# Four edge layers of a graph network: run sums kept as blocks of first runs, written by GpSimd

## The chip, the cores and the metric

One core of a Trainium2 chip runs the whole program in one launch. The metric is the device time of one execution in microseconds (us). Smaller is better.

## The reference, cut to what matters

The network works on 50000 nodes with 256 values each and on 25000 edges (`src`, `dst`), sorted by `dst`. Four sub-networks follow each other, each with a residual and a layer norm: a hypergraph network, two graph-attention layers with four heads, a graph convolution with batch norm, and two more attention layers. An edge layer takes the row of every edge's source, weighs it and sums over all edges with the same target:

```python
alpha = ex / denom[dst]
msg = h[src] * alpha[:, :, None]
out = jax.ops.segment_sum(msg, dst, num_segments=n)
```

Edges with one target lie side by side. Such a stretch is called a run here, and its sum a run sum.

## The kernel before, in words

The edges lie on 128 partitions (`P`), 196 in a row on each (`C`), cut into 25 batches (`NBAT`) of 8 columns (`BC`). The last batch has 4. Five layers have edges: l1, l2 (attention, in the class `Nodes` the kinds `l1a` and `l1b`), l3 (convolution, `gcn`), l5 and l6 (attention, `l3a` and `l3b`). A batch norm stands between l3 and l5.

The class `Edges` does the edges of a layer. GpSimd (POOL) gathers the source rows of a batch, one indirect DMA for each column into one of three buffers `eg` (L1804). VectorE (DVE) weighs them (L2008, in l3 L1995) and adds them up along the partition into one of three buffers `erun` (L2024): element k of a partition is the sum of its run up to k. At the batch's end DVE raises `s_run`. In the attention layers ScalarE (ACT) then copies the running maxima beside the sums (L1876) and raises `s_mc`. SyncE (SP) waits for that and stores the whole batch, 128 partitions by 8 columns, in a DRAM table (L1828): `GSUMS` in l1, l2, l5, `SUMS` in l3, and `GSUMS1` in l6. The buffer is free for a new batch when `s_sv` tells that the store has landed.

A run that goes on from one partition to the next has to be joined. After the last batch, POOL waits for all stores and gathers one row for each partition, the sum of its first run, by the index `repair32` (L1812, tile `hp`). PE multiplies it by a matrix that carries it to the partition before (l3: L1842), and DVE adds it to the last run there (`join`). Nothing else reads the stored sums. A partition whose first run doesn't continue one of the partition before has the index 60000, which is out of bounds, and such rows are left out of a gather or scatter. In the data of the reference 41 of the 128 partitions start inside a run; in 40 of them that run ends within the first 8 columns, in one within the second 8.

The class `Nodes` does the tiles of 512 nodes beside it: 49 that own the targets (region 0) and 49 others (region 1). All engines follow one list of ticks. In a tick POOL first issues what `Edges.gpsimd` gives it, then what `Nodes.gpsimd` gives it, and waits in that order. In l2 and l5 that is a reciprocal square root for two tiles (L2340, tile `rs`). In l5, POOL also has the square roots of the region-1 tiles that are finished in the same layer (L2348, tile `vrs`), which DVE waits for in `moved_shifts` (L2733), and the scatter of their rows to the output (L2356, four for a tile), which wait for ACT to normalize them (`l_v`).

Every layer, and the setup ahead of the first, is a block: no engine starts the next one before all are done. In the setup SP issues loads, the first 40 pieces that clear the table `NS0` (L191), and three stores of zeros (L326, L327), and then waits until these have landed.

```python
for b in range(NBAT):
    if tick == (self.copy_at(b) + 1 if self.heads else self.at(b) + 2):
        if self.heads:
            sp.wait_ge(self.s_mc, b + 1)
        else:
            sp.wait_ge(self.s_run, b + 1)
        sp.dma_start(self.accv[:, b * BC:b * BC + WIDTH[b], :], self.run[b % self.nrun][:, 0:WIDTH[b], :]).then_inc(self.s_sv[b % self.nrun], 16)
```

Of the kernel before, what the change touches and what calls it, by code (L numbers as in the profile page):

```python
# [225 lines left out]
def setup_phase(nc, S, V, A, T, early):  # L226
    with Scope(nc, "su") as s:
# [64 lines left out]
        s_pad = s.sem("pad_rows_ready")  # L292
        s_ps = s.sem("pad_rows_stored")
        with s.block() as block:

            @block.sync
            def _(sp):
# [33 lines left out]
            @block.gpsimd
            def _(pool):
# [56 lines left out]
            def _(dve):  # L389
# [27 lines left out]
                dve.tensor_copy(small[:, 2:3], hpos[:])  # L417
                dve.memset(S["same"][:, 0:1], 0.0)
# [122 lines left out]
                dve.sem_inc(s_cw, 1)  # L541
                dve.memset(S["row_a"][:], 0.0)
# [1160 lines left out]
class Edges:  # L1703


    def __init__(self, nc, S, s, table, tw, index, acc, heads, first, slots, load=None, bias=None):
# [5 lines left out]
        self.aw, self.sumw = acc.shape[1], D + H  # L1712
        self.accv = acc.rearrange("(p c) w -> p c w", c=C)
# [5 lines left out]
        self.s_sv = s.sems("runs_stored", self.nrun)  # L1719
# [1272 lines left out]
```

## Time and profile before

| | |
|---|---|
| median of 3 runs | 6476.59 us (6467.43 to 6479.67) |
| the profiled execution, span from first to last instruction | 6468.6 us |
| PE, DVE, ACT, POOL busy | 4325.2, 4671.1, 3126.0, 3855.5 us |
| l1, batches | 2703 to 3119 us |
| l2, batches | 3266 to 3847 us |
| l3, batches | 3960 to 4325 us |
| l5, batches | 5063 to 5703 us |
| moved by DMA | 1558.35 MB |

The page gives no other time of the profiled execution than its span. The stages run one after another and have different limits, so an engine's share of the whole span tells little. Each stage has to be read by itself: which engine has no idle time there, and what the others wait for.

### The profile page before, as it was taken

How to read it: one execution, taken by the hardware profiler on the slowest of the kernel's cores; microseconds unless marked ns; L12 is line 12 of the kernel's file. 1: busy time of each engine (PE TensorE's matmuls, PEld its weight loads, DVE VectorE, ACT ScalarE, POOL GpSimd, SP SyncE). 2: the span in 40 equal slices, each digit the busy share in tenths (PEclk: the TensorE clock that was granted, in tenths of full speed). 3: DMA queues.
4: the chain of work that ended last, by engine and by line, in shares of the span. 5: the costliest groups of instructions: out<-in, count | busy, mean ns of one | idle time of the engine just before them, and what ended most of it. 6: DMA issues, size and time to landing. Idle time of an engine off the chain costs nothing. (4 is left out here: it accounts for less than half of the span.)

```text
span 6468.6 us, 75458 instructions
## 1 busy us (share of the span) xinstructions
PE 4325.2 (67%) x19189; PEld 3131.7 (48%) x19189; DVE 4671.1 (72%) x15403; ACT 3126.0 (48%) x6788; POOL 3855.5 (60%) x3139
## 2 busy tenths in 40 slices
PE   2668884038886899588876667997898477790000
PEld 1257773037775677477622223555777355560000
DVE  6645454745554877599599986977888899957776
ACT  0023331013332566488655556765776377782333
POOL 4767775767886577666155524741111688747776
PEclk9689997569998899799977778998999788895555
DMA  8845545974443898799688878998998687756665
GB/s 301 311 125 78 79 75 101 388 230 77 79 78 52 288 312 302 243 326 319 222 292 295 304 264 307 399 338 300 342 347 302 213 287 275 276 213 224 236 237 199
DMA packets 616396, 1558.35 MB, mean 241 GB/s; under 512 B 126988, under 2 KB 283090, under 8 KB 599038
## 3 DMA queue, kind: packets, MB, share of 16 engines
q1 hardware_dynamic: 430270, 1159.75, 51.2%
q0 software_dynamic: 185696, 393.77, 22.6%
q8 instruction: 158, 2.59, 0.2%
q14 instruction: 272, 2.23, 0.1%
HBM read 794.19 MB, written 811.66 MB: 248 GB/s over the span
## 5 line engine op out<-in xcount | busy, mean ns | idle before, releaser
L859 POOL DMA_INDIRECT NS<-e_tot,e_idx x392 | 658.9, 1681 | 232.7 <-ACT e_tot L1122 91.6
L1804 POOL DMA_INDIRECT l_eg<-HBT,k_nsrc x392 | 484.4, 1236 | 352.3 <-POOLq L160 120.6
L993 DVE TENSOR_SCALAR e_eq<-e_pk,z_skey 128x128 f32<-128x128 f32 x588 | 203.6, 347 | 621.0 <-DMA NS<-e_tot,e_idx 590.4
L2410 PE MATMUL l_pm<-k_w_L3b,l_zt 128*128 128x258 f32 x1568 | 412.4, 423 | 124.3 <-ACT l_o L2469 123.8
L1257 POOL DMA_INDIRECT XH<-n_o,z_home x392 | 384.3, 980 | 165.0 <-issue 113.1
L2384 PE MATMUL l_ps<-l_a,k_ident 128*128 128x512 f32 x392 | 308.4, 879 | 227.1 <-DVE l_a L2662 215.9
L2548 ACT ACTIVATE l_a<-l_a,l_eshare 128x64 f32<-128x64 f32 (+1 forms) x980 | 280.5, 372 | 311.6 <-DVE l_eshare L2066 311.6
L2024 DVE SCALAR_TENSOR_TENSOR l_erun<-l_erun,k_same,l_eg 128x260 f32<-128x260 f32 (+2 forms) x880 | 415.4, 472 | 3.0
L2410 PEld LDWEIGHTS l_pm<-k_w_L3b,l_zt 128*128 128x128 f32 x1568 | 327.0, 214 | 186.2 <-issue 133.0
L2410 PE MATMUL l_pm<-k_w_L1b,l_zt 128*128 128x264 f32 x1568 | 380.9, 398 | 54.1 <-ACT l_o L2469 53.8
L2739 DVE BATCH_NORM_STATS2 l_bs<-l_a 128x6 f32<-128x256 f32 x1016 | 402.3, 413 | 1.3
L1511 POOL TENSOR_TENSOR n_rs<-n_ve,k_minus_half 128x8 f32<-128x8 f32 x49 | 80.2, 1636 | 520.9 <-DVE n_ve L1669 520.9
L1847 PE MATMUL l_pb<-l_jx,k_ones 128*128 128x128 f32 x26 | 5.2, 351 | 560.7 <-DVE l_jx L2084 560.7
L1068 PE MATMUL e_po<-z_w_e2n,e_hid 128*128 128x256 f32 x1584 | 375.9, 380 | 2.8 <-DVEq L956 2.8
L1077 PE MATMUL e_pr<-e_zt,z_w_n2e 128*128 128x256 f32 x1584 | 377.2, 381 | 0.7 <-ACT e_hid L1142 0.7
L1281 PE MATMUL n_pm<-z_w_L1a,n_zt 128*128 128x264 f32 x1568 | 370.5, 390 | 0.0
L1548 PE MATMUL n_pm<-k_w_L3a,n_zt 128*128 128x264 f32 x1568 | 367.7, 388 | 0.1
L1804 POOL DMA_INDIRECT l_eg<-XH,k_psrc x196 | 255.4, 1303 | 177.9 <-DVEq L2029 119.0
L2497 ACT ACTIVATE l_z<-l_a,l_nb,l_rs 128x256 f32<-128x256 f32 x624 | 321.9, 588 | 78.2 <-DVE l_nb L2803 69.6
L2401 PE MATMUL l_pm<-l_zt,k_w_L 128*128 128x512 f32 x784 | 354.2, 595 | 0.0
L2410 PEld LDWEIGHTS l_pm<-k_w_L1b,l_zt 128*128 128x128 f32 x1568 | 298.3, 195 | 113.2 <-issue 64.6
L1068 PEld LDWEIGHTS e_po<-z_w_e2n,e_hid 128*128 128x128 f32 x1584 | 301.6, 191 | 45.2 <-issue 3.5
(443 smaller groups left out, 13326.7 us busy)
## 6 DMA issues: line engine op xcount, KB each, us to landing
HBT<-l_o SPq DMA_DIRECT2D x196, 528.0 KB, 4.3
l_a<-HBT SPq DMA_DIRECT2D x156, 528.0 KB, 6.2
GSUMS<-l_erun SPq DMA_DIRECT2D x72, 1056.0 KB, 6.0
NS<-z_zero SPq DMA_DIRECT2D x100, 520.0 KB, 5.9
l_a<-XH SPq DMA_DIRECT2D x98, 528.0 KB, 6.1
HA<-n_o SPq DMA_DIRECT2D x98, 528.0 KB, 4.5
l_a<-HA SPq DMA_DIRECT2D x98, 528.0 KB, 6.3
X<-l_z SPq DMA_DIRECT2D x98, 520.0 KB, 7.7
```

The lines of the kernel that those rows point to most:

```text
L859: pool.indirect_dma_start(out=nodes, out_offset=bass.IndirectOffsetOnAxis(ap=idx[q % DEEP][:, k:k + 1], axis=0), in_=tot[q % 2][:, k, :], ...
L1068: mm = pe.matmul(po[:, k, :], hid[q % 2][:, i, k * P:(k + 1) * P], w2[:, i, 0:D], start=i == 0, stop=i == KC - 1)
L1077: mm = pe.matmul(pr[:, n, :], w1[:, i, n * P:(n + 1) * P], zt[q % 2][:, i].rearrange("p j n -> p (j n)"), start=i == 0, stop=i == KC - 1)
L1257: pool.indirect_dma_start(out=T["XH"], out_offset=bass.IndirectOffsetOnAxis(ap=S["home32"][:, col:col + 1], axis=0), in_=o[t % RO][:, j, : ...
L1281: last = pe.matmul(pm[h][:, i, 0:RW], zt[t % 2][:, k, h * (J // 2) + i, :], weight[:, k, :], start=k == 0, stop=k == KC - 1)
L1548: last = pe.matmul(pm[h][:, i, 0:RW], zt[t % 2][:, k, h * (J // 2) + i, :], weight[:, k, :], start=k == 0, stop=k == KC - 1)
L1804: pool.indirect_dma_start(out=self.g[b % self.ng][:, k, :], out_offset=None, in_=self.table, in_offset=bass.IndirectOffsetOnAxis(ap=self.i ...
L2024: lk.link(dve.scalar_tensor_tensor(rt[:, k, 0:n], before, S["same"][:, b * BC + k:b * BC + k + 1], g[:, k, 0:n], ALU.mult, ALU.add))
L2401: last = pe.matmul(self.pm[u % 2][:, m, :], self.weight[:, k, m * P:(m + 1) * P], zt[:, k].rearrange("p j n -> p (j n)"), start=k == 0, st ...
L2410: last = pe.matmul(self.pm[h][:, i, 0:self.wc], zt[:, k, h * (J // 2) + i, :], self.weight[:, k, 0:self.wc], start=k == 0, stop=k == KC - 1)
L2497: last = act.activation(z[:, j, 0:D], a[:, j, 0:D], ACT.Identity, bias=self.nb[b][:, col:col + 1], scale=self.rs[b][:, col:col + 1])
L2739: self.stat_lk.link(dve.bn_stats(bs[:, u % 2 * J + j, :], a[:, j, 0:D]))
```

## The change

In l1, l2, l3 and l5 (`kept=True`) SP no longer stores the batches. For each batch POOL issues one indirect DMA in its place. It writes the 8 columns of a partition, one piece of 8448 bytes (8192 in l3), to row p of a small table (`HEADRUNS`, `HEADSUMS`), for those partitions alone whose first run continues one from the partition before and ends in this batch (`headblock32`). All other indices are out of bounds. The write waits for `s_mc` (in l3 `s_run`), as the store did, and stands in POOL's order ahead of the gathers of its tick. The gather for the join reads the row in that block (`headrow32`). The setup works out the two indices on DVE, and SP clears the two tables at the end of its list, with five more DMAs that the setup waits for. l6 stays as it was.

```diff
@@ setup, SP
                 sp.dma_start(T["SUMS"][PC:PC + 1, :], pad[0:1, 0:D]).then_inc(s_ps, 16)
+                zero = S["zero"][:].rearrange("p r c -> p (r c)")
+                for table in (T["HEADRUNS"], T["HEADSUMS"]):
+                    for c in range(0, table.shape[1], CLEAR * SW):
+                        w = min(CLEAR * SW, table.shape[1] - c)
+                        sp.dma_start(table[:, c:c + w], zero[:, 0:w]).then_inc(s_hz, 16)
                 sp.wait_ge(s_pre, 16)
                 sp.wait_ge(s_ps, 16 * 3)
+                sp.wait_ge(s_hz, 16 * 5)
@@ setup, POOL
+                pool.iota(block32[:], [[BC, NBAT]], base=0, channel_multiplier=0).then_inc(s_iota, 1)
+                pool.iota(part32x[:], [[1, 1]], base=0, channel_multiplier=BC).then_inc(s_iota, 1)
@@ setup, DVE
+                dve.tensor_copy(colblock[:], block32[:])
+                dve.tensor_copy(part8[:, 0:1], part32x[:])
...
+                dve.tensor_scalar(part8[:, 1:2], small[:, 0:1], -1.0, None, ALU.add)
+                dve.tensor_scalar(part8[:, 2:3], small[:, 0:1], float(-BC), None, ALU.add)
+                dve.drain()
...
+                dve.tensor_copy(S["headblock32"][:], colblock[:])
...
+                dve.tensor_scalar(S["headrow32"][:], part8[:, 3:4], float(NONE), None, ALU.add)
@@ class Edges
-        self.aw, self.sumw = acc.shape[1], D + H
-        self.accv = acc.rearrange("(p c) w -> p c w", c=C)
+        self.aw, self.sumw = acc.shape[1] // BC if kept else acc.shape[1], D + H
+        self.kept = kept
+        self.accv = None if kept else acc.rearrange("(p c) w -> p c w", c=C)
...
-        self.s_sv = s.sems("runs_stored", self.nrun)
+        self.s_sv = [s.pool_sem(S, f"head_runs_kept{b}") for b in range(self.nrun)] if kept else s.sems("runs_stored", self.nrun)
...
+    def kept_at(self, b):
+        return self.copy_at(b) + 1 if self.heads else self.at(b) + 2
@@ Edges.gpsimd, in the loop over the batches, behind the gathers of a batch
+            if self.kept and tick == self.kept_at(b):
+                if self.heads:
+                    pool.wait_ge(self.s_mc, b + 1)
+                else:
+                    pool.wait_ge(self.s_run, b + 1)
+                pool.indirect_dma_start(out=self.acc, out_offset=bass.IndirectOffsetOnAxis(ap=self.S["headblock32"][:, b:b + 1], axis=0),
+                                        in_=self.run[b % self.nrun][:].rearrange("p k w -> p (k w)"), in_offset=None,
+                                        bounds_check=P - 1, oob_is_err=False).then_inc(self.s_sv[b % self.nrun], 16)
@@ Edges.gpsimd, the join
-            pool.indirect_dma_start(out=self.hp[:, :], out_offset=None, in_=self.acc,
-                                    in_offset=bass.IndirectOffsetOnAxis(ap=self.S["repair32"][:], axis=0),
-                                    bounds_check=PC - 1, oob_is_err=False).then_inc(self.s_hp, 16)
+            if self.kept:
+                pool.indirect_dma_start(out=self.hp[:, :], out_offset=None, in_=self.acc.rearrange("p (k w) -> (p k) w", k=BC),
+                                        in_offset=bass.IndirectOffsetOnAxis(ap=self.S["headrow32"][:], axis=0),
+                                        bounds_check=P * BC - 1, oob_is_err=False).then_inc(self.s_hp, 16)
...
@@ Edges.sync
-            if tick == (self.copy_at(b) + 1 if self.heads else self.at(b) + 2):
+            if not self.kept and tick == self.kept_at(b):
@@ gnn_kernel
-        "GSUMS": nc.dram_tensor("GSUMS", (PC, RW), F32).ap(),
+        "HEADRUNS": nc.dram_tensor("HEADRUNS", (P, BC * RW), F32).ap(),
+        "HEADSUMS": nc.dram_tensor("HEADSUMS", (P, BC * D), F32).ap(),
```

Line numbers of the changed kernel are larger by some 40 to 52: the gather L1804 is L1843 there, the new write L1852, the gather for the join L1860, and L2340, L2348, L2356 are L2392, L2400, L2408.

POOL in the middle of l5, before (`l_eg` the gathers of edge rows, `l_rs` and `l_vrs` the square roots, `out_dram<-l_v` the scatter to the output):

```order
L2340 TENSOR_TENSOR l_rs<-l_ve,k_minus_half 128x8
L2356 DMA out_dram<-l_v,k_ids 50000x256 x4
L1804 DMA l_eg<-HA,k_nsrc 128x264 x2
L2348 TENSOR_TENSOR l_vrs<-l_vve,k_minus_half 128x8
L2356 DMA out_dram<-l_v,k_ids 50000x256 x4
L1804 DMA l_eg<-HA,k_nsrc 128x264 x2
L2340 TENSOR_TENSOR l_rs<-l_ve,k_minus_half 128x8
L1804 DMA l_eg<-HA,k_nsrc 128x264 x6
L2340 TENSOR_TENSOR l_rs<-l_ve,k_minus_half 128x8
```

The same place in the changed kernel:

```order
L2392 TENSOR_TENSOR l_rs<-l_ve,k_minus_half 128x8
L2408 DMA out_dram<-l_v,k_ids 50000x256 x4
L1852 DMA HEADRUNS<-l_erun,k_headblock 128x2112
L1843 DMA l_eg<-HA,k_nsrc 128x264 x2
L2400 TENSOR_TENSOR l_vrs<-l_vve,k_minus_half 128x8
L2408 DMA out_dram<-l_v,k_ids 50000x256 x4
L1843 DMA l_eg<-HA,k_nsrc 128x264 x2
L2392 TENSOR_TENSOR l_rs<-l_ve,k_minus_half 128x8
L1843 DMA l_eg<-HA,k_nsrc 128x264 x4
L1852 DMA HEADRUNS<-l_erun,k_headblock 128x2112
L1843 DMA l_eg<-HA,k_nsrc 128x264 x2
L2392 TENSOR_TENSOR l_rs<-l_ve,k_minus_half 128x8
```

Two writes have come in, each behind the first two gathers of a batch and ahead of the others. All that follows on POOL stands behind them, the square root `l_vrs` among it.

POOL at the end of l3, before:

```order
L1804 DMA l_eg<-X,k_nsrc 128x260 x196
L1812 DMA l_hp<-SUMS,k_repair 128x256
L2842 UNCONDITIONAL_BRANCH
L1496 UNCONDITIONAL_BRANCH
L1499 TENSOR_TENSOR n_bt<-n_bmv,k_minus_half 128x2
```

And in the changed kernel:

```order
L1843 DMA l_eg<-X,k_nsrc 128x260 x6
L1852 DMA HEADSUMS<-l_erun,k_headblock 128x2048
L1843 DMA l_eg<-X,k_nsrc 128x260 x6
L1852 DMA HEADSUMS<-l_erun,k_headblock 128x2048 x3
L1860 DMA l_hp<-HEADSUMS,k_headrow 128x256
```

The last three writes of the layer stand on POOL right ahead of the gather for the join, where POOL before had nothing but the wait for SP's stores.

## Rows read from the trace of the kernel before

**Rows 1.** Windows by stage (l1, l2, l3, l5): length, busy (instructions), clock, DMA share, GB/s.

```profile
2703.00:3119.00 416.00, 363.49 (x1852) 306.14 (x1851) 408.37 (x850) 346.68 (x944) 226.55 (x169) 0.98 0.94 321
3266.00:3847.00 581.00, 396.13 (x644) 119.16 (x645) 564.74 (x1540) 347.17 (x940) 287.37 (x209) 0.75 0.87 297
3960.00:4325.00 365.00, 365.00 (x1358) 198.94 (x1358) 316.48 (x606) 265.82 (x531) 233.90 (x187) 1.00 1.01 386
5063.00:5703.00 640.00, 478.38 (x2051) 348.41 (x2052) 597.03 (x1864) 439.68 (x949) 497.39 (x365) 0.84 0.78 274
```

**Rows 2.** DMA issues: the run stores that go (count, KB each, us to landing).

```profile
GSUMS<-l_erun SPq DMA_DIRECT2D x72, 1056.0 KB, 6.0
SUMS<-l_erun SPq DMA_DIRECT2D x24, 1024.0 KB, 6.8
...
GSUMS<-l_erun SPq DMA_DIRECT2D x3, 528.0 KB, 4.1
```

**Rows 3.** Groups of POOL's DMAs in l1, l2, l3, l5: busy, mean ns | idle, releasers.

```profile
L1804 POOL DMA_INDIRECT l_eg<-XH,k_psrc x169 | 226.6, 1341 | 146.0 <-DVEq L2029 100.9 <-issue 45.1
L1804 POOL DMA_INDIRECT l_eg<-HBT,k_nsrc x171 | 225.1, 1316 | 152.7 <-DVEq L2029 103.2 <-issue 42.2 <-ACT l_z L2497 7.3
L1804 POOL DMA_INDIRECT l_eg<-X,k_nsrc x172 | 218.1, 1268 | 92.3 <-issue 46.3 <-DVEq L2029 46.0
L1804 POOL DMA_INDIRECT l_eg<-HA,k_nsrc x178 | 224.6, 1262 | 73.0 <-issue 48.6 <-DVEq L2029 23.5 <-ACT l_a L2497 0.9
L2356 POOL DMA_INDIRECT out_dram<-l_v,k_ids x128 | 163.2, 1275 | 47.8 <-issue 34.6 <-ACT l_v L2533 12.9 <-ACT l_a L2497 0.3
```

**Rows 4.** Waits of DVE in l5's batches: us in total, times, longest.

```profile
DVE l_vnb L2733 <- POOL l_vrs L2348: 38.2, 11, 5.7
```

**Rows 5.** Timeline of l5, POOL and DVE: start, duration, [idle before <- releaser].

```profile
5173.09 1.02 POOL L1804 DMA_INDIRECT l_eg<-HA,k_nsrc  x1 [8.59 <-DVEq L2029]
...
5222.02 0.17 DVE L2733 SCALAR_TENSOR_TENSOR l_vnb<-l_vmv,l_vrs 128x8 f32<-128x8 f32 x1 [3.67 <-POOL l_vrs L2348]
...
5392.55 0.17 DVE L2733 SCALAR_TENSOR_TENSOR l_vnb<-l_vmv,l_vrs 128x8 f32<-128x8 f32 x1 [3.66 <-POOL l_vrs L2348]
...
5447.09 1.02 POOL L2356 DMA_INDIRECT out_dram<-l_v,k_ids  x1 [2.69 <-ACT l_v L2533]
...
5513.66 1.02 POOL L1804 DMA_INDIRECT l_eg<-HA,k_nsrc  x1 [2.26 <-DVEq L2029]
...
5631.19 0.17 DVE L2733 SCALAR_TENSOR_TENSOR l_vnb<-l_vmv,l_vrs 128x8 f32<-128x8 f32 x1 [1.36 <-POOL l_vrs L2348]
```

**Rows 6.** The two scatters by `repair32` (L841), 41 of 128 rows: issue to landing.

```profile
DMA to landing us min/median/max: 2.3/3.6/4.8
```

**Rows 7.** The scatter that adds in DRAM, from the page's groups: busy, mean ns.

```profile
L859 POOL DMA_INDIRECT NS<-e_tot,e_idx x392 | 658.9, 1681 | 232.7 <-ACT e_tot L1122 91.6
```

**Rows 8.** Timeline of l3's join on SP, POOL and PE.

```profile
4317.67 0.66 SPq L1828 DMA_DIRECT2D SUMS<-l_erun  x1
...
4325.61 1.00 POOL L1812 DMA_INDIRECT l_hp<-SUMS,k_repair  x1 [35.11 <-DMA SUMS<-l_erun]
...
4323.93 1.04 PE L2440 MATMUL l_pt<-k_ident,l_a 128*128 128x128 f32 x8
...
4328.24 1.04 PE L2440 MATMUL l_pt<-k_ident,l_a 128*128 128x128 f32 x8
4331.95 0.70 PE L1842 MATMUL l_pc<-l_hp,k_joinT 128*128 128x256 f32 x2 [2.67 <-DMA l_hp<-SUMS,k_repair]
...
4337.61 1.04 PE L2440 MATMUL l_pt<-k_ident,l_a 128*128 128x128 f32 x8
```

**Rows 9.** The setup's end: a window by its DMA, SP's last store, DVE's next instruction.

```profile
80.00:94.00 14.00, 0.00 (x0) 0.00 (x0) 4.11 (x13) 0.00 (x0) 0.00 (x0) 1.00 1.03 410
...
96.63 0.21 SPq L327 DMA_DIRECT2D SUMS<-su_pad  x1
...
106.27 0.91 DVE L877 MEMSET e_run<- 128x1024 f32 x1 [21.62 <-PEq L160]
```

More of the change, by code:

```diff
@@ L541, in _ @@
                 dve.sem_inc(s_cw, 1)
+                dve.tensor_scalar(part8[:, 1:2], small[:, 0:1], -1.0, None, ALU.add)
+                dve.tensor_scalar(part8[:, 2:3], small[:, 0:1], float(-BC), None, ALU.add)
+                dve.drain()
+                dve.tensor_scalar(inblock[:], colblock[:], part8[:, 1:2], None, ALU.is_le)
+                dve.tensor_scalar(colblock[:], colblock[:], part8[:, 2:3], small[:, 3:4], ALU.is_ge, ALU.mult)
+                dve.tensor_scalar(part8[:, 4:5], part8[:, 0:1], 1.0 / BC, float(-NONE), ALU.mult, ALU.add)
+                dve.drain()
+                dve.tensor_tensor(inblock[:], inblock[:], colblock[:], ALU.mult)
+                dve.drain()
+                dve.tensor_scalar(colblock[:], inblock[:], part8[:, 4:5], float(NONE), ALU.mult, ALU.add)
+                dve.drain()
+                dve.tensor_copy(S["headblock32"][:], colblock[:])
+                dve.tensor_tensor(inblock[:], inblock[:], V["iota"][:, 0:NBAT], ALU.mult)
+                dve.drain()
+                dve.tensor_reduce(part8[:, 3:4], inblock[:], AX_X, ALU.add)
+                dve.tensor_tensor(part8[:, 1:2], part8[:, 1:2], part8[:, 0:1], ALU.add)
+                dve.drain()
+                dve.scalar_tensor_tensor(part8[:, 3:4], part8[:, 3:4], float(-BC), part8[:, 1:2], ALU.mult, ALU.add)
+                dve.drain()
+                dve.tensor_scalar(part8[:, 3:4], part8[:, 3:4], float(-NONE), small[:, 3:4], ALU.add, ALU.mult)
+                dve.drain()
+                dve.tensor_scalar(S["headrow32"][:], part8[:, 3:4], float(NONE), None, ALU.add)
                 dve.memset(S["row_a"][:], 0.0)
@@ L1703, with __init__ @@
 class Edges:
-    def __init__(self, nc, S, s, table, tw, index, acc, heads, first, slots, load=None, bias=None):
+    def __init__(self, nc, S, s, table, tw, index, acc, heads, first, slots, load=None, bias=None, kept=False):
         self.bias, self.s_ad = bias, s.sem("target_logits_biased")
@@ L1811, in gpsimd @@
                 pool.wait_ge(self.s_sv[b], 16 * len(range(b, NBAT, self.nrun)))
-            pool.indirect_dma_start(out=self.hp[:, :], out_offset=None, in_=self.acc,
-                                    in_offset=bass.IndirectOffsetOnAxis(ap=self.S["repair32"][:], axis=0),
-                                    bounds_check=PC - 1, oob_is_err=False).then_inc(self.s_hp, 16)
+            if self.kept:
+                pool.indirect_dma_start(out=self.hp[:, :], out_offset=None, in_=self.acc.rearrange("p (k w) -> (p k) w", k=BC),
+                                        in_offset=bass.IndirectOffsetOnAxis(ap=self.S["headrow32"][:], axis=0),
+                                        bounds_check=P * BC - 1, oob_is_err=False).then_inc(self.s_hp, 16)
+            else:
+                pool.indirect_dma_start(out=self.hp[:, :], out_offset=None, in_=self.acc,
+                                        in_offset=bass.IndirectOffsetOnAxis(ap=self.S["repair32"][:], axis=0),
+                                        bounds_check=PC - 1, oob_is_err=False).then_inc(self.s_hp, 16)
     def landed(self, b):
@@ L2951, in gnn_kernel @@
         layer_phase(nc, S, "l1", dict(kind="l1a", rows=h1, rw=RW, weight=S["w_L1b"], out=T["HBT"], self_act=2, slots=FIRST),
-                    dict(table=pairs, tw=RW, index=S["psrc32"], acc=T["GSUMS"], load=asd), first=12)
+                    dict(table=pairs, tw=RW, index=S["psrc32"], acc=T["HEADRUNS"], kept=True, load=asd), first=12)
         layer_phase(nc, S, "l2", dict(kind="l1b", rows=T["HBT"], rw=RW, resid=x1, out=T["X2"], self_act=2, slots=FIRST),
-                    dict(table=T["HBT"], tw=RW, index=S["nsrc32"], acc=T["GSUMS"], bias=S["logit_b"]), first=12)
+                    dict(table=T["HBT"], tw=RW, index=S["nsrc32"], acc=T["HEADRUNS"], kept=True, bias=S["logit_b"]), first=12)
         with Scope(nc, "y") as y:
```

11 lines of the change are left out of this document (7 added, 4 removed).

## The prediction, on record before the run

> **What bounds the kernel now.** I read the windows by stage first, since the change touches four stages with different limits. In l1 VectorE (DVE) works 408.37 of 416 us and in l2 564.74 of 581; in l3 the matmul engine (PE) works 365 of 365 [rows 1]. These three have an owner that hardly ever rests. In l3 the beat shows it: from one tile's transposes to the next, 4323.93 to 4328.24, are 4.31 us [rows 8].
>
> l5 is different. DVE has 597.03 us of work in 640, and GpSimd (POOL) 497.39 [rows 1]; but POOL also spends 48.6 and 34.6 us on issuing between its DMAs [rows 3], so it is taken for 580.6 of 640 us. The waits say who waits for whom: DVE stood 38.2 us, 11 times, for a square root on POOL [rows 4]. The timeline shows the loop. POOL gets its last long rest at 5173.09 (8.59 us); from then on DVE waits for it again and again, first at 5222.02, last at 5631.19. The same wait, 3.67 and 3.66 us long, comes back after 5392.55 - 5222.02 = 170.5 us, which is six batches. In such a period POOL itself rests only twice, 2.69 us for ScalarE (ACT) and 2.26 us for the end of a batch on DVE, and both are echoes of its own lateness [rows 5]. So from 5173 to 5631 the chain that sets the pace runs mostly through POOL's list.
>
> DMA is the third view. The stores that go are 72 x 1056 KB and 24 x 1024 KB [rows 2], some 103 MB of the 1558 MB moved. The DMA share is 0.94 in l1 and 1.01 in l3 [rows 1], yet DVE in l1 and PE in l3 don't stop for DMA within the batches. Only at the end of l3 does PE wait for one [rows 8].
>
> **The change, part by part.** What it removes: 25 stores in each of four layers. None of them is waited for before the join, so in the batches they are worth 0. The bound below is the 7.6 us of l1 in which DVE is idle and the 16.3 us of l2, if all of it were made by crowded loads; I take 0, since an owner that is busy 97% and more leaves its rests to other causes too.
>
> What it adds in l1, l2 and l3: one indirect DMA on POOL per batch, with the gathers of the next batch behind it. A scatter costs 1275 ns in l5 plus 34.6/128 = 0.27 us of issuing [rows 3], so 1.55 us. POOL's rests for the end of a batch are 100.9, 103.2 and 46.0 us over some 21 batches [rows 3], that is 4.8, 4.9 and 2.2 us per batch. Each is larger than 1.55, so the write fits in: 0. If the cover failed it would fail first in l3, by at most 25 x 0.5 = 12 us if the price were 2.7. In l1 and l2 the write also waits for ACT's copy of the maxima, and POOL's gathers behind it; this eats rest of the same kind.
>
> l5: here the writes come on top of a full list. By the order rows each stands behind the first two gathers of a batch, and twice between one `l_vrs` and the next. From 5173 to 5631 are 458 us, or 458/170.5 x 6 = 16 batches, so 16 writes. One of six, the one just ahead of the 2.69 us rest, is swallowed by it; that happens three times. The other 13 push `l_vrs`, DVE behind it and the next batch behind DVE: 13 x 1.55 = **+20.1 us**. From below: a price of 1.02 + 0.27 = 1.29 us (the short scatter at 5447.09 [rows 5]), 16.8 us for 13, and if the rests of 2.69 (three) and 2.26 (two) could all be filled, 12.6 less, 4.2. From above: all 16 at the price of the scatter that adds, 1681 ns [rows 7], plus 0.27: 31.2. I take 20.1, by the rows of the same stage.
>
> A scatter's length is not its own. In l5 its mean is 1275 ns, a quarter above the 1.02 us of a short one [rows 3, 5]; what lengthens the others is left open here, and the mean carries it into the sum. The Trainium skill (SBUF — State Buffer, Who interferes with whom) says that a DMA issued from SP is free of DVE, while GpSimd, which writes descriptors itself, is kept out by some DVE instructions. By its figure for a blocked one, about 3.1 us, 13 writes would cost an estimated 13 x 3.4 = 44 us. The rows of l5 don't show such a mean, so the sum stays with them.
>
> The join of l3: the last store is issued at 4317.67, and POOL's gather starts at 4325.61 [rows 8], 7.9 us later. The write would be issued at about the same moment, since both wait for the same semaphore, and land 3.6 us later (2.3 to 4.8) [rows 6]. The gather then comes some 4 us earlier, more than the 2.67 us that PE waits for it. The tile in which PE waits takes 4337.61 - 4328.24 = 9.37 us in place of 4.31, and PE has no slack to make it up: **-5.1 us**, 0 at the least. In the joins of l1, l2 and l5 the half batch's store lands in 4.1 us [rows 2] against 3.6 [rows 6]: 0, from -2 to +1 together.
>
> The setup: DVE is done long before its end and rests 21.62 us up to 106.27 [rows 9], so its extra arithmetic is hidden, and ends later only if it took longer than that. What DVE waits for is SP's list of clears. SP's last store stands at 96.63; the DMA engines move 410 GB/s ahead of it, which is all they reach in this program's stages. The five new clears are 128 x (2112 + 2048) x 4 = 2.13 MB behind that: 2.13/410 = **+5.2 us**, with nothing beside it. At l1's 321 GB/s it would be 6.6; if the last transfers' tail hid part, 3.
>
> **The sum**: +20.1 - 5.1 + 5.2 = +20.2 us on the profiled span of 6468.6, so 6488.8. The median of the runs shown, 6476.59, lies 8 us above that span; with the same difference the forecast is **6497 us**.
>
> **The rivals.**
>
> *POOL's rests take the writes.* If the 2.69 and 2.26 us are room and no echo, l5 costs 4 to 10 us and the time is 6476.6 + 5.2 + 7 - 5.1 = 6484: no change that can be told. For it: DVE itself is idle for 43 us in l5, so neither engine is full. Against it: DVE's wait and POOL's rest follow each other in the same period, as links of one chain. It decides when l5 grows by less than 13.
>
> *Traffic is what paces the stages* (this one ends faster). If loads and gathers arrive late because 1 MB stores crowd them, l3 would shorten by its stores' 25 MB at 386 GB/s, 65 us, or by any part of it; with a tenth of that and 10 us from l1 and l2 the sum is 6476.6 + 20.2 - 6.5 - 10 = 6480, and from a quarter of l3's on with l1's and l2's idle time the kernel is faster: 6476.6 + 20.2 - 16 - 24 = 6457. The Trainium skill (SBUF — State Buffer, A bandwidth-pool intuition that's wrong) holds that HBM is almost always the bottleneck from end to end. The shares of 0.94 and 1.01 speak for it. Against it stand the owners' full windows and the beat of 4.31 us.
>
> *The list of POOL gets longer than planned.* At 1681 ns for each write and with l3's POOL falling behind, 6476.6 + 5.2 + 31 + 5 = 6518. The price of a scatter whose rows are nearly all out of bounds is not in the trace by itself.
>
> *The writes do next to nothing.* Should an indirect DMA without a valid row be skipped in well under 1 us, l5 costs under 8 us: 6482.
>
> **How the numbers follow.** A measurement of this kernel can tell about 0.2% (13 us) from no change. The forecast gets 0.50 (6489 to 6509), the longer list 0.14, both slower. POOL's rests 0.22 and the cheap write 0.04: same. The traffic 0.10: faster. That is slower 0.64, same 0.26, faster 0.10. The range of 6470 to 6518 leaves out most of the faster case and the far end of the longer list.
>
> **What would show it.** In the changed profile: SP's run stores gone and some 100 MB less moved; POOL's new group of 25 for each layer, at 1.0 to 1.6 us; in l5 DVE's wait for `l_vrs` well above 38.2 us and the six-batch period near 178 us in place of 170.5; in l3 PE's beat unbroken at the join; the first DVE instruction of the next block near 111.5. The prediction is wrong if l5's period stays at 170 us, if the writes take under 0.7 us or over 2, or if l1 or l2 change by more than 5 us.

## The result, and the profile after

The changed kernel takes 6487.07 us (median of 15 runs, 6474.70 to 6489.53). The kernel before, beside it and with 15 runs too, takes 6467.43 us. The ratio is 1.0027 (95% interval 1.0020 to 1.0034), so the change costs 19.6 us by the medians and 13 to 22 us by the interval. Forecast were 6497 us and +20.2 us: slower, as expected, and by the expected amount. The 10 us between 6497 and 6487 are nearly all the starting point: the three runs known then had a median of 6476.59, fifteen have 6467.43. But the right sum hides a wrong term and one that was not seen, and these are what this part is about.

The profiled execution has a span of 6483.0 us against 6468.6. It splits by the first VectorE (DVE) instruction of each block. (A second profile of the kernel before stands in the table, to show how far two profiles of one kernel differ. The columns are us, the differences are taken before rounding, and the forecast is by stage.)

| stage | before | before, again | after | after - before | forecast |
|---|---|---|---|---|---|
| setup | 106.3 | 106.7 | 111.3 | +5.0 | +5.2 |
| hypergraph layers, first nodes | 2541.5 | 2549.6 | 2543.7 | +2.3 | 0 |
| l1 | 565.4 | 563.4 | 569.9 | +4.6 | 0 |
| l2, to l3's first tile | 746.0 | 746.0 | 744.6 | -1.5 | 0 |
| l3 | 428.0 | 429.2 | 422.8 | -5.2 | -5.1 |
| batch norm | 647.0 | 647.2 | 646.6 | -0.4 | 0 |
| l5 | 793.4 | 790.3 | 801.6 | +8.1 | +20.1 |
| l6 | 641.0 | 641.8 | 642.6 | +1.5 | 0 |

The unchanged second stage took between 2529 and 2551 us in the twelve profiles of this case, so a few us there say nothing. l3 with the write in it and the batch norm repeat to 1 us, l2 to some 6 (744.1 to 750.2). l1 falls into two groups: 563.4 to 566.1 us in the four profiles in which it stores, 569.7 to 570.1 in the eight in which it writes.

The windows by stage, as in [rows 1] (length, then busy time of PE, PEld, DVE, ACT, POOL, clock, DMA share, GB/s):

```profile
2711.00:3127.00 416.00, 365.86 (x1856) 308.49 (x1856) 408.78 (x850) 346.83 (x940) 269.98 (x195) 0.97 0.83 260
3279.00:3860.00 581.00, 395.57 (x643) 118.90 (x643) 563.46 (x1538) 345.97 (x937) 310.45 (x233) 0.75 0.79 252
3970.00:4335.00 365.00, 365.00 (x1357) 198.98 (x1356) 318.20 (x607) 264.97 (x530) 252.65 (x213) 1.00 0.96 316
5064.00:5717.00 653.00, 475.89 (x2059) 347.65 (x2060) 599.32 (x1874) 441.56 (x952) 519.88 (x392) 0.84 0.67 223
```

The stores are gone: in l1 the DMA rate falls from 321 to 260 GB/s, in l3 from 386 to 316. The owners of l1 to l3 do the same work in the same length. PE is busy 365 of 365 us in l3 with or without 25 MB of stores, so the traffic did not pace that stage. Only l5's stretch is longer, 653 us for the 640 of before, with DVE's work unchanged.

The groups of POOL's DMAs, as in [rows 3] (busy, mean ns | idle before them, what ended it), of l1, l2, l3 and, from the fourth row on, l5:

```profile
L1852 POOL DMA_INDIRECT HEADRUNS<-l_erun,k_headblock x25 | 35.8, 1431 | 46.1 <-ACT l_erun L1928 40.0 <-issue 6.1
...
L1852 POOL DMA_INDIRECT HEADRUNS<-l_erun,k_headblock x25 | 37.0, 1481 | 55.9 <-ACT l_erun L1928 53.3 <-issue 2.6
...
L1852 POOL DMA_INDIRECT HEADSUMS<-l_erun,k_headblock x25 | 30.9, 1238 | 50.5 <-DVEq L2081 47.2 <-issue 3.4
...
L1843 POOL DMA_INDIRECT l_eg<-HA,k_nsrc x180 | 217.9, 1210 | 65.1 <-issue 48.5 <-DVEq L2081 14.2 <-ACT l_erun L1928 1.5
L1852 POOL DMA_INDIRECT HEADRUNS<-l_erun,k_headblock x25 | 33.6, 1343 | 7.3 <-issue 7.0 <-ACT l_a L2549 0.3
```

In l1 to l3 the writes took over the rest that the gathers had: POOL now waits ahead of the write (40.0, 53.3 and 47.2 us). In l5 there is no rest ahead of them; a write costs 1.343 + 7.0/25 = 1.62 us of the list, against 1.55 forecast. The gathers got shorter, 1262 to 1210 ns.

DVE's waits for POOL's square root in l5 rose from 38.2 us [rows 4] to 50.6, and the timeline has the loop of [rows 5] again:

```profile
DVE l_vnb L2785 <- POOL l_vrs L2400: 50.6, 11, 7.0
```

```profile
5225.44 0.17 DVE L2785 SCALAR_TENSOR_TENSOR l_vnb<-l_vmv,l_vrs 128x8 f32<-128x8 f32 x1 [5.33 <-POOL l_vrs L2400]
...
5281.20 1.02 POOL L2408 DMA_INDIRECT out_dram<-l_v,k_ids  x1 [2.18 <-ACT l_v L2585]
...
5349.15 1.02 POOL L1843 DMA_INDIRECT l_eg<-HA,k_nsrc  x1 [2.27 <-DVEq L2081]
...
5399.78 0.17 DVE L2785 SCALAR_TENSOR_TENSOR l_vnb<-l_vmv,l_vrs 128x8 f32<-128x8 f32 x1 [5.32 <-POOL l_vrs L2400]
```

The period of six batches is 5399.78 - 5225.44 = 174.3 us (170.5 before, some 178 forecast). POOL's two rests are still there, 2.18 and 2.27 us for 2.69 and 2.26. They took in 0.5 us of six writes, so in the main they were echoes, as forecast; but the first of them was also forecast to swallow one whole write of six, and it did not.

Setup and l3's join, the timelines that answer to [rows 9] and [rows 8]:

```profile
101.19 1.83 SPq L335 DMA_DIRECT2D HEADSUMS<-z_zero  x2
...
111.26 0.91 DVE L912 MEMSET e_run<- 128x1024 f32 x1 [24.90 <-PEq L160]
...
4327.91 0.98 POOL L1852 DMA_INDIRECT HEADSUMS<-l_erun,k_headblock  x1 [5.61 <-DVEq L2081]
...
4333.34 1.04 POOL L1860 DMA_INDIRECT l_hp<-HEADSUMS,k_headrow  x1 [4.46 <-issue]
...
4338.57 1.04 PE L2492 MATMUL l_pt<-k_ident,l_a 128*128 128x128 f32 x8
...
4339.45 0.60 PE L1894 MATMUL l_pc<-l_hp,k_joinT 128*128 128x256 f32 x2
...
4343.31 1.04 PE L2492 MATMUL l_pt<-k_ident,l_a 128*128 128x128 f32 x8
```

The next block starts 5.0 us later. In l3 PE no longer waits: the tile of the join takes 4343.31 - 4338.57 = 4.74 us in place of 9.37, the 4.31 of the beat and the join's own 0.4. The 4.6 us that this saves are more than the wait of 2.67. In the kernel before, PE's granted clock stood at the lower of its two levels (0.50 of full speed, 1.2 of 2.4 GHz) behind that wait, and the tile's eight large matmuls took 5.29 us; with no wait they take the 3.60 of every other tile, at a clock of 1.00. Before, the window's columns being length, PE busy, clock, DMA share and GB/s:

```profile
4332.48 5.29 PE L2401 MATMUL l_pm<-l_zt,k_w_L 128*128 128x512 f32 x8
...
4334.00:4336.00 2.00, 2.00 (x3) 0.50 0.01 5
```

So some 1.7 us of the gain are the clock's. (before_again has the same: a wait of 2.91 us, the clock at 0.50 behind it, and 9.43 us for the tile.) The gather starts 5.4 us after the last write, where it started 7.9 after the last store. That is 2.5 us sooner and not the 4 of the forecast. It also lands sooner, 3.0 us after its start for 6.3 before, and the two together took away the whole wait.

What was not forecast shows in l1's join. First before, then after (the gather of the first runs, and the first DVE instruction that reads it):

```profile
3115.97 0.32 SPq L1828 DMA_DIRECT2D GSUMS<-l_erun  x1
3119.78 1.00 POOL L1812 DMA_INDIRECT l_hp<-GSUMS,k_repair  x1 [44.24 <-DMA GSUMS<-l_erun]
3122.87 0.28 DVE L2084 TENSOR_SCALAR l_jx<-k_ident,l_hp 128x128 f32<-128x128 f32 x1 [4.07 <-DMA l_hp<-GSUMS,k_repair]
```

```profile
3123.32 0.98 POOL L1852 DMA_INDIRECT HEADRUNS<-l_erun,k_headblock  x1 [9.61 <-ACT l_erun L1928]
3128.70 1.05 POOL L1860 DMA_INDIRECT l_hp<-HEADRUNS,k_headrow  x1 [4.40 <-issue]
3133.89 0.29 DVE L2136 TENSOR_SCALAR l_jx<-k_ident,l_hp 128x128 f32<-128x128 f32 x1 [7.04 <-DMA l_hp<-HEADRUNS,k_headrow]
```

From the last write to the gather are 5.4 us where the store took 3.8, and from the gather to its reader 5.2 where it was 3.1, though the write moves far less than the store and the gather fetches the same 41 rows. Counted from the start of the stage, the last write is issued at the moment of the last store (468.3 and 468.2 us), and the reader runs 3.8 us later.

### The profile page after: what moved, and what is told of

Same layout as the page of the kernel before. It is cut to its first block and busy times, and to the rows that moved or that the text cites. A ratio compares the mean times of both kernels' runs of the same rounds, so it can differ in the third digit from the quotient of the medians.

```text
span 6483.0 us, 75578 instructions
## 1 busy us (share of the span) xinstructions
PE 4323.5 (67%) x19189; PEld 3138.3 (48%) x19189; DVE 4676.3 (72%) x15419; ACT 3125.2 (48%) x6788; POOL 3959.3 (61%) x3241
## 5 line engine op out<-in xcount | busy, mean ns | idle before, releaser
L1843 POOL DMA_INDIRECT l_eg<-HBT,k_nsrc x392 | 468.4, 1195 | 343.3 <-POOLq L160 123.3
L1843 POOL DMA_INDIRECT l_eg<-XH,k_psrc x196 | 262.3, 1338 | 130.6 <-DVEq L2081 71.4
```

The source lines that it names most:

```text
L1843: pool.indirect_dma_start(out=self.g[b % self.ng][:, k, :], out_offset=None, in_=self.table, in_offset=bass.IndirectOffsetOnAxis(ap=self.i ...
```

## The experiments

Three theories on l5 were told apart first. **List**: the price is the write's length on POOL's list. **Stores**: the writes cost that, but the stores had lengthened POOL's DMAs and held up its gathers, and their removal gave some back. **Slots**: how long a DMA on POOL takes depends on what DVE does at that moment, and a write takes a long place from a gather. In the tables l5 is cut into the head (to DVE's first use of `l_vrs`), the loop (to its 15th), the way to the join, and the tail. The experiments ran in three sets, each beside runs of the kernel before on the same chip: the first four below, the next four, the last two. The kernel before had a median of 6467.43 us with the changed kernel, and 6456.80, 6479.14 and 6460.54 in the three sets, so between sets only ratios are compared.

### Without 23 of the writes: two_writes_l5

```diff
-            if self.kept and tick == self.kept_at(b):
+            if self.kept and b < self.upto and tick == self.kept_at(b):
...
-                    dict(table=T["HA"], ... acc=T["HEADRUNS"], kept=True))
+                    dict(table=T["HA"], ... acc=T["HEADRUNS"], kept=True, upto=2))
...
```

(The waits for the writes that are gone went with them.)

> l5 issues its write for the first two batches alone (only there does any index lie in range with this data); the other 23 writes and all of l5's stores are gone. Three theories on why l5 grew by 12 us and not by 20. List: a write costs its own length and issue on GpSimd, and nothing else came back; then the six-batch period is that of before, 170.5 us, and the gathers' mean in l5 1.26 us. Stores: the 1 MB stores had lengthened GpSimd's other DMAs, and their removal gave 3 us per period back; then the period is 167 us, the gathers' mean 1.20, and l5 ends 8 to 9 us sooner than before. Slots: a long DMA goes with what VectorE does at that moment, and a write takes such a moment from a gather; then the period is 170.5 again. Time: 6474 (List, Slots), 6465 (Stores).

### Writes and stores: both_l5

```diff
+            if self.toov is not None and tick == self.kept_at(b):
+                sp.wait_ge(self.s_mc, b + 1)
+                sp.dma_start(self.toov[:, b * BC:b * BC + WIDTH[b], :], self.run[b % self.nrun][:, 0:WIDTH[b], :]).then_inc(self.s_too[b % self.nrun], 16)
...
```

> l5 keeps its 25 writes, and SyncE stores the batches as well, as before the change, to a table nobody reads. Stores: GpSimd's gathers in l5 get longer again (1.26 us) and the six-batch period goes from 174.2 to some 177.5 us; time 6495. Slots and List: the period stays at 174.2 and the time at 6487.

### Each write twice: doubled_l5

```diff
+                if self.again is not None:
+                    pool.indirect_dma_start(out=self.again, ...).then_inc(self.s_ag[b % self.nrun], 16)
...
```

> Each of l5's 25 writes is issued twice, the second time to a table nobody reads. It measures the price of one more write at the margin. List: 6 x 1.62 = 9.7 us per period, so 184; Slots and Stores: a short DMA with its issue, 6 x 1.3 = 7.8, so 182; the rival that GpSimd's two rests take writes: at most 2.2 + 2.2 us of it are swallowed, so 178.

### l5 stores again: stored_l5

```diff
-                    dict(table=T["HA"], ... acc=T["HEADRUNS"], kept=True))
+                    dict(table=T["HA"], ... acc=T["GSUMS"]))
```

> l5 goes back to SyncE's stores; l1, l2 and l3 keep the writes. All theories: the six-batch period is 170.5 us again and l5 as long as before, so the time is 10 to 13 us below that of the change, 6475; l1, l2 and l3 repeat what they did in the change (the join of l3 4.6 us shorter, that of l1 some 3 us longer if that was no accident).

What the four gave, with the other runs' profiles beside them (us; the periods are the first and the second six batches of the loop; join wait is DVE's in l5):

| kernel | stores | writes | head | loop | periods | to the join | tail | l5 | join wait |
|---|---|---|---|---|---|---|---|---|---|
| before | 25 | 0 | 127.9 | 469.2 | 170.5, 168.7 | 77.0 | 119.4 | 793.4 | 3.8 |
| before_again | 25 | 0 | 127.8 | 467.8 | 170.5, 168.6 | 76.0 | 118.7 | 790.3 | 2.8 |
| stored_l5 | 25 | 0 | 128.1 | 467.3 | 169.9, 167.4 | 76.0 | 119.0 | 790.5 | 2.8 |
| after | 0 | 25 | 124.9 | 481.3 | 174.3, 174.1 | 77.0 | 118.5 | 801.6 | 3.8 |
| both_l5 | 25 | 25 | 128.7 | 482.2 | 174.6, 174.5 | 80.9 | 119.2 | 811.0 | 7.6 |
| two_writes_l5 | 0 | 2 | 124.8 | 463.5 | 167.3, 167.5 | 73.1 | 118.0 | 779.4 | 0.0 |
| doubled_l5 | 0 | 50 | 127.9 | 503.5 | 182.5, 183.7 | 80.7 | 118.6 | 830.7 | 7.4 |

The ratios: two_writes_l5 1.0008 (0.9998 to 1.0017), both_l5 1.0042 (1.0025 to 1.0059), stored_l5 1.0013 (1.0004 to 1.0023); doubled_l5 has one run, 6505.46 us. The rows behind the periods, of two_writes_l5, both_l5, stored_l5 and doubled_l5 in this order:

```profile
5209.13 0.17 DVE L2789 SCALAR_TENSOR_TENSOR l_vnb<-l_vmv,l_vrs 128x8 f32<-128x8 f32 x1 [2.31 <-POOL l_vrs L2404]
...
5376.48 0.17 DVE L2789 SCALAR_TENSOR_TENSOR l_vnb<-l_vmv,l_vrs 128x8 f32<-128x8 f32 x1 [2.30 <-POOL l_vrs L2404]
```

```profile
5214.01 0.17 DVE L2794 SCALAR_TENSOR_TENSOR l_vnb<-l_vmv,l_vrs 128x8 f32<-128x8 f32 x1 [5.34 <-POOL l_vrs L2409]
...
5388.63 0.17 DVE L2794 SCALAR_TENSOR_TENSOR l_vnb<-l_vmv,l_vrs 128x8 f32<-128x8 f32 x1 [5.33 <-POOL l_vrs L2409]
```

```profile
5388.26 0.17 DVE L2785 SCALAR_TENSOR_TENSOR l_vnb<-l_vmv,l_vrs 128x8 f32<-128x8 f32 x1 [3.67 <-POOL l_vrs L2400]
...
5555.68 0.17 DVE L2785 SCALAR_TENSOR_TENSOR l_vnb<-l_vmv,l_vrs 128x8 f32<-128x8 f32 x1 [2.30 <-POOL l_vrs L2400]
```

```profile
5218.86 0.17 DVE L2794 SCALAR_TENSOR_TENSOR l_vnb<-l_vmv,l_vrs 128x8 f32<-128x8 f32 x1 [8.13 <-POOL l_vrs L2409]
...
5401.39 0.17 DVE L2794 SCALAR_TENSOR_TENSOR l_vnb<-l_vmv,l_vrs 128x8 f32<-128x8 f32 x1 [8.12 <-POOL l_vrs L2409]
```

What follows. In the loop 16 writes cost 482.2 - 467.3 = 14.9 us with the stores in both kernels (0.93 each) and 481.3 - 463.5 = 17.8 with them in neither (1.11 each). A second write right behind each costs 503.5 - 481.3 = 22.2, 1.39 each. All of these lie below the 1.62 us that a write takes on POOL's list. Over the whole of l5 the writes cost 811.0 - 790.5 = 20.5 and 801.6 - 779.4 = 22.2 us; most of what the loop does not explain is on the way to the join (80.9 against 76.0, 77.0 against 73.1). There two_writes_l5 has no late write or store left to wait for, so its wait of 0.0 is its own. The doubled writes speak against the rests: the periods are 182.5 and 183.7 us, for a forecast of 178 if the rests took writes in, 182 for Slots and Stores, 184 for List.

And l5 gains when the stores go: 11 to 14 us without the writes (779.4 against 790.3 to 793.4), 9.4 with them (811.0 against 801.6). These are single profiles. That of two_writes_l5 is its fastest execution of ten, 6453.00 us for a median of 6461.59, and the medians of the same set put stored_l5 only 5.1 us above it (6466.71) and both_l5 17.3 above stored_l5 (6484.05). By the medians, then, the stores are worth some 5 us without the writes. With them it is some 10 (the ratios 1.0042 and 1.0027), and the writes cost 17 with the stores and 12 without (1.0027 and 1.0008). The ratio of two_writes_l5 is nearer to the forecast of List and Slots (6474, a ratio of 1.0010), its period of 167.3 and 167.5 us to that of Stores (167). In both_l5 it is the other way round: the ratio is nearer to that of Stores (6495, 1.0043), the period to that of List and Slots.

Where the gain is differs. 3 to 4 us lie in the head, in each pair: 124.7 to 124.9 in the four profiles without stores and with at most one write a batch, 127.8 to 128.7 in the five that store as before. (doubled_l5 has 127.9 for another reason: its waits for gathers are as short as in the changed kernel, and a wait of 2.6 us for POOL has come in.) This repeats, so List, by which the stores are worth nothing, falls. In the loop Stores falls in its own form: with the writes there, stores change it by 0.9 us (without them by 4 to 6), the gathers are no longer (1196 ns in both_l5, 1210 after), and the short period of 167.4 us also came up in stored_l5, with its stores. A last part, 3 to 4 us, is at the join, whose wait has two lengths, 2 to 4 us or 7 to 8, in kernels of either kind. What picks one was not found.

**Slots** is seen in the trace itself. One gather of the loop stands at the same place in two periods of the kernel before (5222.02 + 13.5 and 5392.55 + 13.5), and takes 2.48 us in one and 1.29 in the other:

```profile
5234.62 1.22 DVE L2645 TENSOR_TENSOR l_a<-l_a,l_part 128x1024 f32<-128x1024 f32 x1
5235.50 2.48 POOL L1804 DMA_INDIRECT l_eg<-HA,k_nsrc  x1 [0.30 <-issue]
...
5235.86 1.22 DVE L2008 TENSOR_TENSOR l_eg<-l_eg 128x1024 f32<-128x1024 f32 x1
...
5405.21 1.21 DVE L2645 TENSOR_TENSOR l_a<-l_a,l_part 128x1024 f32<-128x1024 f32 x1
...
5406.01 1.29 POOL L1804 DMA_INDIRECT l_eg<-HA,k_nsrc  x1 [0.30 <-issue]
5406.44 1.21 DVE L2008 TENSOR_TENSOR l_eg<-l_eg 128x1024 f32<-128x1024 f32 x1
```

Both start while a long DVE instruction runs. The second ends at 5407.30, 0.88 us after that instruction (5406.42); the first lets the next one pass too and ends at 5237.98, 0.90 after 5237.08. The gap between the two DVE instructions is 0.02 us, and to catch it or not is worth 1.22 us. In the kernel before 128 of l5's 305 DMAs on POOL with a record start within such an instruction (a TENSOR_TENSOR of over 0.3 us): they take 1531 ns in the mean, and 116 of them end between 0.8 and 1.0 us after it (the median of all is 0.89); the other 177 take 1077. That it is DVE's instruction that holds the DMA is read from these times; no run moved one of them to try it. The period follows the lengths: the two of stored_l5 differ by 2.5 us, their gathers and scatters by 2.4 (109.4 and 107.0). By Slots, a write that lands in such a moment is long in place of the gather that would have been. In one period, first before, then after (groups of POOL from 5222.0 to 5392.5 and from 5225.4 to 5399.8):

```profile
L1804 POOL DMA_INDIRECT l_eg<-HA,k_nsrc x48 | 60.9, 1268 | 15.8 <-issue 13.2 <-DVEq L2029 2.3 <-ACT l_a L2497 0.3
L2356 POOL DMA_INDIRECT out_dram<-l_v,k_ids x40 | 49.6, 1241 | 13.8 <-issue 10.9 <-ACT l_v L2533 2.9
```

```profile
L1843 POOL DMA_INDIRECT l_eg<-HA,k_nsrc x48 | 56.5, 1177 | 15.8 <-issue 12.9 <-DVEq L2081 2.3 <-ACT l_erun L1928 0.3
L2408 POOL DMA_INDIRECT out_dram<-l_v,k_ids x40 | 48.2, 1206 | 13.3 <-issue 10.6 <-ACT l_v L2585 2.4 <-ACT l_a L2549 0.3
...
L1852 POOL DMA_INDIRECT HEADRUNS<-l_erun,k_headblock x6 | 8.8, 1474 | 1.8 <-issue 1.8
```

Six writes and their issues take 10.6 us of the list; the gathers and scatters take 5.8 less. The period grew by 3.8. But not all of the 5.8 is the writes' doing. The same period of two_writes_l5, with neither writes nor stores:

```profile
L1843 POOL DMA_INDIRECT l_eg<-HA,k_nsrc x48 | 59.1, 1231 | 15.8 <-issue 13.2 <-DVEq L2085 2.3 <-ACT l_a L2553 0.3
L2412 POOL DMA_INDIRECT out_dram<-l_v,k_ids x40 | 47.8, 1196 | 13.8 <-issue 10.8 <-ACT l_v L2589 2.7 <-ACT l_a L2553 0.3
```

Its gathers and scatters take 106.9 us, those of before 110.5, those of after 104.7. Against it the writes shorten them by 2.2 us and the period grows by 7.0. The other 3.6 us were gone before a write came in; the ten periods with stores lie between, at 107.0 to 110.5.

### The kernel before, again: before_again

> The kernel before, once more, for a profile from the chip that ran the variants. All theories: no difference to the kernel before beside it. It shows how far the same stage differs between two profiles of one kernel (2 to 4 us in the setup's neighbour stages and l6 if the drifts seen there are none of the change's), and whether its six-batch period in l5 is always 170.5 us or also 167.4, as it was once in stored_l5 and in both periods of two_writes_l5. Stores: 170.5 in both. Slots (a DMA on GpSimd ends 0.9 us after a long VectorE instruction, and slips in between two of them or not): between 167.4 and 170.5, not always the same.

Ratio 1.0001 (0.9991 to 1.0010). The periods were 170.5 and 168.6: Slots, not always the same. Over ten periods with stores and no writes they lie at 167.4 to 170.5, over the eight with the writes where they stand in the change (after, both_l5, clears_moved, sp_hold_l5) at 174.1 to 174.6. Whether stores make the long ones more frequent stays open: without either there are but two, both 167.4.

### The clears off the setup's end: clears_moved

```diff
-                        sp.dma_start(table[:, c:c + w], zero[:, 0:w]).then_inc(s_hz, 16)
-                sp.wait_ge(s_hz, 16 * 5)
...
+                    if listing and tick == 3:
...
+                                sp.dma_start(table[:, c:c + w], zero[:, 0:w]).then_inc(S["head_cleared"], 16)
```

> The change, with the five DMAs that clear the two tables issued in the next block, where SyncE has little to do, in place of the setup's end. My theory: the next block starts 5 us sooner than in the change (its first VectorE instruction near 106.3 in place of 111.3), nothing later moves, and the ratio to the kernel before falls from 1.0027 to 1.0019. Rival: the setup waits for something else by then, such as the index arithmetic, and gives less than 2 us back.

```profile
106.20 0.91 DVE L905 MEMSET e_run<- 128x1024 f32 x1 [19.89 <-PEq L160]
```

Ratio 1.0018 (1.0009 to 1.0027), and the block starts at 106.20. The five clears were the whole of the setup's 5 us.

### Writes in l3 alone: l3_only

```diff
-                    dict(table=pairs, ... acc=T["HEADRUNS"], kept=True, load=asd), first=12)
+                    dict(table=pairs, ... acc=T["GSUMS"], load=asd), first=12)
...
```

> Writes in l3 alone; l1, l2 and l5 store as before, and the one table left is cleared in the next block. My theory: l3's join keeps its 4.6 us, the setup ends near 106.3 (only the index arithmetic is left there), l1's join is back at 4.1 us of waiting, l5 is that of before: 4 to 5 us below the kernel before, ratio 0.9993. Rival (the stores' traffic paces l1 and l2): slower than stored_l5 with its clears taken off, by what l1 and l2 lose.

Ratio 0.9996 (0.9987 to 1.0005). l3 takes 422.8 us, as in all ten profiles with the write there (422.7 to 422.9; 428.0 and 429.2 without), l5 791.3. l1's join waits 4.4 us. Over all profiles that wait is 2.8 to 4.4 us with stores in l1 (four) and 6.9 to 8.5 with writes (eight), so the 3 to 5 us there belong to the change. Why was not tried. The rival is not excluded: against stored_l5 l1 takes 5.4 us less here, but l2 5.9 more (750.2), and a ratio whose interval holds 1.0000 does not show the gain of 4 to 5 us as a whole.

### The writes behind the square roots: late_l5

```diff
                     nodes.gpsimd(pool, tick, out_end)
+                    edges.gpsimd_late(pool, tick)
...
```

(The write of the last batch keeps its place.)

> The change, but in l5 each write stands behind the square roots and output scatters of its tick in place of ahead of them. List: the same chain runs through GpSimd's list wherever the write stands, so the six-batch period stays at 174 to 175 us. Rival (the place costs, since a write ahead of the square root makes VectorE wait): the period falls to some 169 to 171. Slots: it moves by multiples of 1.2 us up or down.

Both periods are 172.9 us and the loop 479.6; ratio 1.0021 (1.0012 to 1.0030). That is 1.3 us below the change, about one of Slots' steps, and between List's 174 to 175 and the rival's 169 to 171: the place is worth 1.7 us of the 12 to 13 that the loop grew. The rest stays wherever the write stands.

### SyncE waits but does not store: sp_hold_l5

At the head of l5 SP's list shows what the store held up. Before, and after (eight of the loads in one row):

```profile
5033.80 0.80 SPq L2283 DMA_DIRECT2D l_a<-HA  x2
...
5063.14 0.32 SPq L1828 DMA_DIRECT2D GSUMS<-l_erun  x1
5063.50 3.28 SPq L2283 DMA_DIRECT2D l_a<-HA  x4
```

```profile
5038.55 4.03 SPq L2335 DMA_DIRECT2D l_a<-HA  x8
```

Before, SP issued two loads, then stood 28 us at the wait of the first store, and its next loads left together with that store.

```diff
+            if self.hold and tick == self.kept_at(b):
+                sp.wait_ge(self.s_mc, b + 1)
```

> The change, but in l5 SyncE still waits for the copied maxima of each batch where it issued the store before; it stores nothing. At the head of l5 the change is 3 us ahead of every kernel that stores there (the first wait of VectorE for a square root comes 125 us after the block's start in place of 128). Hold theory: SyncE's list stood 29 us behind that first wait, with only two loads issued, so the loads came late and met the gathers; then the hold alone brings 128 back, and the time is 3 us above the change. Traffic theory: the stores' bytes delayed the gathers; then the head stays at 125. The six-batch period should stay at 174 to 174.6 by both.

The head takes 126.0 us, between the two forecasts: of the 3 us of after (124.9) against 128, the hold makes 1.1, and the other 2 go with the store itself. DVE's first two waits for gathers there show which is which, first before, then with the hold alone:

```profile
5060.87 0.17 DVE L1967 COPY l_ex<-l_em 128x4 f32<-128x4 f32 x1 [4.76 <-DMA l_eg<-HA,k_nsrc]
...
5075.79 0.17 DVE L1967 COPY l_ex<-l_em 128x4 f32<-128x4 f32 x1 [2.82 <-DMA l_eg<-HA,k_nsrc]
```

```profile
5065.38 0.17 DVE L2021 COPY l_ex<-l_em 128x4 f32<-128x4 f32 x1 [4.74 <-DMA l_eg<-HA,k_nsrc]
...
5078.32 0.17 DVE L2021 COPY l_ex<-l_em 128x4 f32<-128x4 f32 x1 [0.83 <-DMA l_eg<-HA,k_nsrc]
```

After, the waits are 3.16, 0.61 and 0.76 us. With the hold the first is as long as before; the second is short as soon as nothing is stored. The periods are 174.4 and 174.1. The ratio is 1.0035 (1.0021 to 1.0048), l5's join having its long wait (7.2 us).

### Writes in l2 and l3 alone, two first stores later: l23_lag

```diff
-            if not self.kept and tick == self.kept_at(b):
+            if not self.kept and tick == self.kept_at(b) + (self.lag if b == 0 else 0):
...
+                    dict(table=T["HA"], ... acc=T["GSUMS"], lag=4))
...
+                    dict(table=T["HBT"], ... acc=T["GSUMS1"], lag=4))
...
```

> A version put together from the findings: writes in l2 and l3 alone, l1, l5 and l6 store; the tables are cleared in the next block; in l5 and l6 the first batch's store stands four ticks later in SyncE's list, behind more loads. Expected against the kernel before: the setup 0, l1 0, l2 -1 to -2.5, l3's join -5, l5's head -3 by the hold theory (0 by the traffic theory), l6's head between -3 and 0; together 9 to 13 us, ratio 0.9980 to 0.9986. Rival: l6 or l5 wait for the late store with their third buffer and give it back.

6448.44 us against 6460.54 of the kernel before beside it: ratio 0.9982 (0.9973 to 0.9991), 12 us faster, as expected. Not all is from where it was expected: l2 differs by 1.2 us, less than it varies by (744.8 for 746.0), l3 gives 5 to 6 (422.7), the head of l5 1.5 (126.3, the first wait still 4.7 us and the second 0.8, as with the hold), but l5's join has its long wait (7.1) and takes that back (l5 794.2). l6 takes 637.8 us, where the other eleven profiles have 640.2 to 647.2; how much of that the later store brings was not tried by itself.

## Why the prediction was right, and where it was not

- **The sign and the size**: slower by 20.2 us forecast, by 19.6 measured. The mark of the first rival was met, since l5 grew by less than 13 us, but not for its reason: POOL's rests took in 0.5 us of six writes. The cheap write did not come: it takes 1.343 us.
- **The starting point**: "the same difference" between span and median was put at 8 us from three runs. The runs listed for the changed kernel are all some 2 us above their spans, so the median of three stood some 6 us above the execution in the profile; it stood 9.2 above the median of fifteen.
- **The setup, +5.2**: right, and by its cause: 5.0 us, gone when the clears moved. (The other profiles with the clears at that place have 110.2 to 111.2, so 3.5 to 5.)
- **l1, l2, l3 in the batches, 0**: right; the writes filled POOL's rests.
- **l3's join, -5.1**: right in size, and the mechanism held in its main step, that PE no longer waits: 9.37 us became 4.74, and ten profiles repeat it. Inside it two things differ from what was told. The write's landing was priced at 3.6 us and the gather started 5.4 after it, which on its own would not have removed PE's wait; the gather's faster landing did the rest. And of the 5.1 us, 1.7 were PE at the lower clock and 0.4 the join's own work, which stays.
- **The joins of l1, l2 and l5, "0, from -2 to +1 together"**: wrong for l1. It was priced by a landing of 3.6 us against 4.1. The 3.6 is the midpoint of two landings, 2.3 and 4.8 us, at moments when DMA moved 14 and 33 GB/s; at l1's join it moved 291. In l1 the write took 5.4 us to the gather's start, and the gather 2.1 us more to its reader. l2's join wait fell from 5.2 to 4.0. l5's stayed at 3.8 here.
- **l5, 13 x 1.55 = +20.1**: wrong in three of its parts. The first is "One of six ... is swallowed": no rest swallowed one, all 16 writes count. The second is the price of 1.55 us each, which took the list's time for the stage's: the loop pays 0.93 to 1.11 us for a write, 14.9 to 17.8 in all, in part since gathers and scatters get shorter as writes come in (2.2 us in a period of six). The third is "What it removes: ... in the batches they are worth 0": removing the stores gave 9 to 14 us of l5 back by the profiles (5 to 10 by the medians), at its head, at its join (whose two lengths of wait may be chance) and, between kernels without writes, in the loop. So l5 grew by 8 to 11. The head was open to see in the profile: DVE waited 4.8 and 2.8 us for gathers there, and SP's list had the store's wait ahead of the loads. That two writes stand between one `l_vrs` and the next is true of three places only, but the sum did not use it.
- **The length of a write**: 1.343 us and 0.28 of issue were measured for 1.275 and 0.27. By the estimate of 44 us from the Trainium skill's figure for a blocked one, about 3.1 us (SBUF — State Buffer, A bandwidth-pool intuition that's wrong), l5 would have grown by some four times what it did; no row shows such a mean, as the prediction held.
- **Traffic** as a rival is right in l5's head, by some 2 us; whether the 4 to 6 us of the loop without writes are of its kind stays open. It did not pace l3: the beat stayed at 4.31 us with 386 and with 316 GB/s.
- **"The prediction is wrong if ... l1 or l2 change by more than 5 us"**: l1 changed by 4.6 to 6.6 against the two profiles of before, so that mark was touched.

That the time came out at +19.6 while l5 gave 8 to 11 is thus partly luck: l1's 5 us were not in the sum, and some 5 us lie between the profile (14.4) and the medians (19.6), within the spread of the unchanged stages. stored_l5 has such a gap too: +8.4 us by its ratio, at most 4 by its setup, l1, l2, l3 and l5. Where it arises was not found.

## What to carry to other kernels

A store that nobody waits for can still cost, here some 3 us of l5: it stands in the issuing engine's list, with its wait, ahead of loads that somebody needs, and it shows at the start of a stage, where the windows of the whole stage hide it. An engine whose busy time and issue gaps fill a stage is the wrong place for a new instruction, even for a write of 1.3 us; what the stage pays for it need not be its length (here 0.9 to 1.1 us): measure the price by adding it twice and by taking it away, in kernels that differ in nothing else, and by the medians as well as by one profile. And a change that touches several stages should be split by stage when it is done; here the best version keeps it in two of four.

## What the runs showed of the hardware that was not expected

- An indirect DMA on POOL that starts while a long two-input instruction runs on DVE ends 0.89 us after that instruction (median of 128 in l5), or lets a second one pass where they follow each other by 0.02 us. In the pair shown its length jumps by some 1.2 us by this, and l5's period moves with such lengths (169.9 and 167.4 in one profile). The Trainium skill (SBUF — State Buffer, Who interferes with whom) has a DVE instruction with two SBUF inputs contend with what GpSimd reads there, and infers that descriptor generation is not held by it. The trace shows the indirect DMA held as a whole; such a DMA also reads its indices (`k_nsrc` in its row), and which of the two is held no run here shows.
- A write without one row in range is not skipped and not cheaper: in l5 the batches after the second, all of whose rows are out of range, take 0.97 to 2.49 us on POOL, like a gather.
- Two small transfers in a row, write and gather, can take longer to land than a store of 528 KB and the gather: 10.6 us against 6.9 in l1's join.
